# Three-pass expert products in the first layer of a four-layer kernel, with the rounding on VectorE and the rests on GpSimd

## The reference

```python
x = x + _L0_attn_ref(xn, Wqkv, Wproj, bproj, q_scale, k_scale) + _L0_ffn_ref(xn, gate_w, gate_b, expert_w, expert_b)

# in _L0_ffn_ref: combine_w[t, e] is a token's weight for an expert, 0 where it wasn't chosen
expert_out = jnp.einsum('td,edh->teh', x, expert_w) + expert_b[None, :, :]
out = jnp.einsum('te,teh->th', combine_w, expert_out)
```

## Time and profile before

| | before |
|---|---|
| median of 3 runs (lowest to highest) | 1739.81 us (1737.31 to 1744.27) |
| the profiled execution | 1742.57 us |
| its span on the core | 1740.8 us |
| PE busy over the span | 1638.6 us (94%) |
| DVE busy | 1012.4 us (58%) |
| ACT busy | 843.1 us (48%) |
| POOL busy | 396.0 us (23%) |

### The profile page before, as it was taken

One profiled execution on the slowest core, in us unless ns is written; L12 is line 12 of the kernel. 1 busy time (PEld: TensorE's weight loads), 2 busy tenths in 40 slices (PEclk: granted clock), 3 DMA queues, 4 the chain that ended last, 5 costly groups with the idle time before them and its releaser, 6 DMA issues. The chain is left out here.

```text
span 1740.8 us, 22780 instructions
## 1 busy us (share of the span) xinstructions
PE 1638.6 (94%) x8686; PEld 986.4 (57%) x8686; DVE 1012.4 (58%) x1655; ACT 843.1 (48%) x1058; POOL 396.0 (23%) x313
## 2 busy tenths in 40 slices
PE   7799999999889999999999999999999997989887
PEld 4232223223545657877878787877878673434433
DVE  4655555553665454465555555555554547898996
ACT  5667777776434443333434333334434343544543
POOL 1000000000553223030211203030111202755553
PEclk8799999999889999999999999999999998999998
DMA  2322222222107620000000000000000001000000
GB/s 81 52 49 49 50 49 50 50 50 82 47 4 184 154 53 1 2 1 2 1 2 1 1 1 1 2 1 1 1 1 1 1 1 44 1 12 7 6 13 13
DMA packets 20698, 48.78 MB, mean 28 GB/s; under 512 B 1200, under 2 KB 2096, under 8 KB 19824
## 3 DMA queue, kind: packets, MB, share of 16 engines
q1 hardware_dynamic: 20592, 47.34, 11.5%
HBM read 44.84 MB, written 2.36 MB: 27 GB/s over the span
## 5 line engine op out<-in xcount | busy, mean ns | idle before, releaser
L537 ACT ACTIVATE probs<-ps 128x1024 f32<-128x1024 f32 x256 | 245.9, 1024 | 88.1 <-PE ps L793 85.1
L2002 PEld LDWEIGHTS ps_o<-v,probs 128*128 128x128 f32 x2048 | 236.3, 192 | 32.7 <-issue 32.7
L2002 PE MATMUL ps_o<-v,probs 128*128 128x129 f32 x2048 | 246.3, 277 | 1.7 <-ACT probs L1682 1.3
L1682 ACT ACTIVATE probs<-ps_ring 128x1024 f32<-128x1024 f32 x128 | 126.2, 1024 | 197.1 <-PE ps_ring L1983 196.8
L807 PE MATMUL ps<-probs,v 128*32 128x512 f32 x1024 | 136.9, 608 | 0.9 <-DVE o_sb L614 0.9
L1675 ACT ACTIVATE xn<-ps_ring,pack 128x512 f32<-128x512 f32 x64 | 40.6, 685 | 156.6 <-PE ps_ring L1519 156.6
L2195 POOL TENSOR_TENSOR rs<-r,state 128x512 f32<-128x512 f32 x64 | 86.8, 1358 | 92.0 <-DVE state L2363 90.7
L1785 DVE RECIPROCAL rden<-ps_o 128x2 f32<-128x2 f32 x128 | 21.4, 167 | 143.8 <-PE ps_o L2002 143.8
L1772 DVE TENSOR_REDUCE negmax<-ps_ring 128x2 f32<-128x1024 f32 x80 | 94.9, 1219 | 15.2 <-PE ps_ring L1950 15.2
L793 PEld LDWEIGHTS ps<-q_stack,k_stack 32*128 32x128 f32 x512 | 31.5, 185 | 123.5 <-issue 96.2
L2363 DVE TENSOR_TENSOR_SCAN state<-decay,state,kv 128x511 f32<-128x511 f32 x64 | 96.8, 1513 | 6.9 <-issue 1.6
(11 more groups left out here) (423 smaller groups left out, 3436.1 us busy)
## 6 DMA issues: line engine op xcount, KB each, us to landing
cwb<-combine_by_expert SPq DMA_DIRECT2D x8, 2048.0 KB
score<-score_by_expert SPq DMA_DIRECT2D x15, 1024.0 KB, 7.8
pack<-pack_dram SPq DMA_DIRECT2D x1, 3840.0 KB, 15.2
x<-x_in SPq DMA_DIRECT2D x2, 1024.0 KB, 6.0
out<-x SPq DMA_DIRECT2D x8, 256.0 KB, 2.0
pack<-pack_dram SPq DMA_DIRECT2D x1, 1543.0 KB, 6.5
pack<-pack_dram SPq DMA_DIRECT2D x1, 1140.0 KB, 9.3
pack<-pack_dram SPq DMA_DIRECT2D x1, 1088.0 KB, 5.1
```

What stands on the lines that cost most here:

```text
L537: nc.scalar.activation(probs[n % 3][:, 2 * half:2 * half + 2, :], ps, ACT.Exp, scale=float(HD0) ** -0.5).then_inc(read, 1)
L1682: nc.scalar.activation(probs[:, n % 2, m, :, :], ps, ACT.Exp).then_inc(read, 1)
L2002: last = nc.tensor.matmul(ps_o[:, i, k * (D + 1):(k + 1) * (D + 1)], probs[:, (b * PAIRS + p) % 2, m, j, queries], v[:, m, h, :], start=(m ...
```

## The change

From batch 1 on:

- The eight expert products of a batch become three float32r passes each (`split_products`). They stand in twos, in the steps 9, 11, 13 and 15, where there was one in each of the steps 8 to 15.
- The expert weights are split once: ACT copies them rounded (`expert_high`, 128x1024), POOL subtracts (`expert_low`).
- The weighed tokens are split for each product: DVE multiplies and rounds (`xe_high`), in its old places; POOL multiplies again unrounded (into `xe[:, 0]`) and subtracts the rounded part (`xe_low`). Both have four buffers, where `xe` had three.
- The output projection of the batch before moves from step 6 to step 7, ahead of the mean squares.
- The bias product counts in `xe_used` like the others; the load of the next routing weights waits for that count alone.

In batch 0 the products stay as they were.

```diff
@@ sync
                 if b:
-                    sp.wait_ge(xe_ready, b * E0_TRUE)
-                    sp.wait_ge(biased, b)
+                    sp.wait_ge(xe_used, b * (E0_TRUE + 1))
@@ gpsimd
-            for b in range(B):
+
+            def square_qk(b):
                 was_read(pool, ("qk", b))
                 nc.gpsimd.tensor_tensor(sq[:, :, :], qk[:, :, :], qk[:, :, :], ALU.mult).then_inc(squared, 1)
+
+            def rest_of_weighed(b, e):
+                n = b * E0_TRUE + e
+                if e == 0:
+                    pool.wait_ge(cw_loaded, b * 32 + 32)
+                nc.gpsimd.tensor_tensor(xe[:, 0, :], xn[:, at(b)], cwb[:, e, :], ALU.mult)
+                pool.drain()
+                pool.wait_ge(xe_high_ready, n - E0_TRUE + 1)
+                pool.wait_ge(xe_used, used(n - 4))
+                nc.gpsimd.tensor_tensor(single(xe_low[:, n % 4, :]), xe[:, 0, :], xe_high[:, n % 4, :], ALU.subtract).then_inc(xe_ready, 1)
+                pool.drain()
+
+            square_qk(0)
+            pool.wait_ge(exp_out, 1)
+            nc.gpsimd.tensor_tensor(single(expert_low[:, :]), w["expert0"], expert_high[:, :], ALU.subtract).then_inc(padded, 1)
+            for b in range(B):
+                if b + 1 < B:
+                    square_qk(b + 1)
+                for e in range(E0_TRUE if b else 0):
+                    rest_of_weighed(b, e)
@@ scalar
             first_rms(0)
             first_rms(1)
+            nc.scalar.activation(single(expert_high[:, :]), w["expert0"], ACT.Copy).then_inc(exp_out, 1)
             act.wait_ge(exp_in, 1)
@@ vector, weigh
-                if n >= 3:
-                    dve.wait_ge(xe_used, n - 2)
-                nc.vector.tensor_tensor(xe[:, n % 3, :], xn[:, at(b)], cwb[:, e, :], ALU.mult).then_inc(xe_ready, 1)
+                if b == 0:
+                    if n >= 3:
+                        dve.wait_ge(xe_used, used(n - 3))
+                    nc.vector.tensor_tensor(xe[:, n % 3, :], xn[:, at(b)], cwb[:, e, :], ALU.mult).then_inc(xe_ready, 1)
+                else:
+                    dve.wait_ge(xe_used, used(n - 4))
+                    nc.vector.tensor_tensor(single(xe_high[:, n % 4, :]), xn[:, at(b)], cwb[:, e, :], ALU.mult).then_inc(xe_high_ready, 1)
@@ vector, route_probs
-                dve.wait_ge(exp_out, 1)
+                dve.wait_ge(exp_out, 2)
@@ tensor, expert
                 pe.wait_ge(xe_ready, n + 1)
-                nc.tensor.matmul(ps_y[:, :], w["expert0"][:, e * P:(e + 1) * P], xe[:, n % 3, :],
-                                 start=(e == 0), stop=False).then_inc(xe_used, 1)
+                cols = slice(e * P, (e + 1) * P)
+                if b == 0:
+                    nc.tensor.matmul(ps_y[:, :], w["expert0"][:, cols], xe[:, n % 3, :], start=(e == 0), stop=False).then_inc(xe_used, 1)
+                    return
+                if n == E0_TRUE:
+                    pe.wait_ge(padded, 5)
+                split_products(nc, ps_y[:, :], (expert_high[:, cols], expert_low[:, cols]), (xe_high[:, n % 4, :], xe_low[:, n % 4, :]),
+                               start=(e == 0), stop=False).then_inc(xe_used, 1)
@@ tensor, the order
-                    if b and s == 6:
+                    if b and s == 7:
                         output(b - 1)
...
                     if b:
-                        if s >= 8:
+                        if s >= 9 and s % 2 == 1:
+                            expert(b, s - 9)
                             expert(b, s - 8)
```

More of the change, by code:

```diff
@@ L419, in layer0_mix @@
         cwT = sb("cwT", [E0_TRUE, T])
-        xe = sb("xe", [P, 3, T])
+        xe, xe_high, xe_low = sb("xe", [P, 3, T]), sb("xe_high", [P, 4, T]), sb("xe_low", [P, 4, T])
+        expert_high, expert_low = (sb(f"expert0_{part}", [P, E0_TRUE * P]) for part in ("high", "low"))
         lg, rank = sh["logits0"], sb("rank0", [P, NT, E0])
@@ L438, in layer0_mix @@
         o_copied, on_ready = sem("o_copied"), sem("on_ready")
-        xe_ready, xe_used = sem("xe_ready"), sem("xe_used")
+        xe_high_ready, xe_ready, xe_used = sem("xe_high_ready"), sem("xe_ready"), sem("xe_used")
         y_done, x_added = sem("y_done"), sem("x_added")
-        cw_loaded, biased = sem("cw_loaded"), sem("biased")
+        cw_loaded = sem("cw_loaded")
         logits_done, exp_in, exp_out, combined, turned, cw_ready, cw_stored = (
@@ L447, in layer0_mix, with used @@
         block = ctx.enter_context(nc.Block())
+        def used(n):
+            return n // E0_TRUE * (E0_TRUE + 1) + n % E0_TRUE + 1
         def bank1(n):
@@ L825, in expert @@
                 pe.wait_ge(xe_ready, n + 1)
-                nc.tensor.matmul(ps_y[:, :], w["expert0"][:, e * P:(e + 1) * P], xe[:, n % 3, :],
-                                 start=(e == 0), stop=False).then_inc(xe_used, 1)
+                cols = slice(e * P, (e + 1) * P)
[6 more added lines that the diff above has]
+                               start=(e == 0), stop=False).then_inc(xe_used, 1)
             def expert_bias(b):
                 pe.wait_ge(cw_loaded, b * 32 + 32)
-                nc.tensor.matmul(ps_y[:, :], w["expert0_b"][0:E0_TRUE, :], cwT[:, :], start=False, stop=False).then_inc(biased, 1)
+                nc.tensor.matmul(ps_y[:, :], w["expert0_b"][0:E0_TRUE, :], cwT[:, :], start=False, stop=False).then_inc(xe_used, 1)
             def output(b):
```

## The result

The changed kernel takes 1786.38 us in the median of four executions (1764.71 to 1796.86), the kernel before 1741.51 beside it: 1.022 times the time before, interval 1.018 to 1.026 (the ratio leaves out the execution of 1796.86, which stands over 1.5% above the fastest). The forecast was 1760 with a range of 1746 to 1772; the sign was right, the size was not. The profiled execution took 1785.23 us with a span of 1783.4 and a mean granted clock of TensorE of 0.949 (before: 0.966). The execution of 1764.71 us had 0.963, and that is a first hint: the executions differ by how much of the time TensorE ran at its lower clock.

A forecast was written before the change was run, and what follows sets the result against it. PE sets the pace only by a little, with ACT full in steps 8 to 12. Six batches at +2.6 us, +3.0 for the last and +1.7 at the start gave 20.3 us, median 1760, range 1746 to 1772.

The forecast's parts named there:

- part 5: End of the batch: DVE and POOL take turns on SBUF tiles, bringing the batch to +2.6 us.
- the sum: Whole kernel: 6 x 2.6 + 3.0 + 1.7 = 20.3 us slower, median 1760 us.
- Part 1: Expert products, batches 1 to 7: three passes save 17.6 us of PE's work, counting only where PE ends last.
- Part 2: Output projection moved from step 6 to 7: ACT's work up to step 12 comes 0.54 us late.
- Part 3: Experts in twos, steps 8 to 13: ACT sets this stretch, PE's saving is gone, +0.17 us a batch so far.
- Part 4: Steps 14 and 15: POOL's chain to expert 7 makes them 8.5 us where they took 7.53, +1.0 a batch.
- The value 0 for the divide chain: POOL's multiplication for expert 0 beside DVE's divide chain: 0 taken, from a range of 0 to 1.13 us a batch.
- the rival of the divide chain: POOL's multiplication for expert 0 also holds up DVE's divide chain: +1.13 x 7 = 8 us, time 1768; chance 0.14.
- Part 6: Once only: start of attention +1.7 us behind POOL's rest of the weights, last batch paced by POOL +3.0 us.
- Nothing collides: POOL and DVE run side by side in the batches: 8.4 us slower, time 1748; chance 0.13.
- It cancels: Collisions are met by gaps and a faster last batch offsets the batch ends: about 1740; chance 0.06.
- PE's work is what counts: ACT's stretch caught up and POOL's rests in time: 17.6 us come off, time 1722; chance 0.05.

The follow-up runs named there:

- experiment 7: Changed kernel's order with fp32 products of unrounded weighed tokens, no rests and no POOL work in the steps: 1755.46 us, 1.0094 of the kernel before.
- experiment 2: Changed kernel without POOL's rests, the second pass multiplying a tile of zeros: 1744.85 us, 1.0023 of the kernel before.
- 6: Changed kernel with POOL fills in place of its products, plus zero-weight passes on PE ahead of experts 5 and 7: 1763.28 us, 1.0126 of the kernel before.
- 1: Changed kernel plus nine zero-weight PE passes a batch, ahead of experts 5 and 7, where PE waits: 1772.76 us, 1.0178 of the kernel before.
- experiment 8: Changed kernel without POOL's rests, with the output projection back in step 6: 1741.86 us, 1.0025 of the kernel before.
- experiment 12: Kernel before, with only mean squares moved to step 5 and ACT's root steps after steps 5 to 8: 1751.76 us, 1.0075 of the kernel before.
- experiment 5: Changed kernel with both POOL instructions per product replaced by fills of about the same length that read nothing: 1771.52 us, 1.0201 of the kernel before.
- experiment 4: Changed kernel with POOL's rest of the expert weights moved from the start to the begin of batch 1: 1777.88 us, 1.0206 of the kernel before.
- experiment 3: Changed kernel with DVE weighing experts 6 and 7 ahead of the copy of the attention sum: 1764.92 us, 1.012 of the kernel before.
- experiment 9: Changed kernel with one three-pass product in each of steps 8 to 15 and the projection in step 6: 1766.27 us, 1.0181 of the kernel before.

## Why the prediction was wrong in size

For batches 1 to 6, in sums over the six, the steps from one kernel to the next read as a ladder:

| | six batches, us | step |
|---|---|---|
| before | 269.1 | |
| twos and the projection in step 7, fp32 (7) | 276.3 | +7.2 |
| three passes without rests (2) | 271.3 | -5.0 |
| rests without collisions but the cast's (6 less its added passes, by its shortest batch: 6 x 46.3) | 277.8 | +6.5 |
| collisions of DVE and POOL (1, by its shortest batch: 6 x 47.92) | 287.5 | +9.7 |
| the clock (the changed kernel) | 303.9 | +16.4 |

The last step holds all that is left, 0.9 us of another cause among it (part 5); so the clock's share is 14 to 15.5 us.

**The step that failed** is the sum itself: it left the granted clock out. The last part of the prediction named a fall of it in the new wait as something that "would add to it and isn't in the sum", with no price, no chance and no rival of its own. It turned out the largest term: 14 to 15.5 us in batches 1 to 6, and 10.5 - 4.0 = 6.5 or less in batch 7. Without it, the terms measured are 2.5 at the start, 18.4 in the six batches (287.5 - 269.1) and about 4.0 in the last (47.7 - 42.3 - 1.4), 24.9 together against the 20.3 of the sum. On the time before, that is about 1766, and the execution of 1764.71 us at a clock of 0.963 stands there (no trace of it is kept). The rows for a price were at hand in the trace of the kernel before, in batch 0. Two windows, steps 11 to 13 of batch 0 and batches 1 to 7, and PE in time in steps 11 and 12 of batch 0:

```profile
81.00:91.30 10.30, 8.11 (x24) 2.20 (x28) 5.23 (x7) 5.95 (x7) 0.00 (x0) 0.50 0.43 68
102.40:413.70 311.30, 301.38 (x1816) 90.61 (x1812) 158.47 (x188) 238.97 (x248) 11.36 (x6) 1.00 0.27 48
```

```profile
79.44 0.50 PE L793 MATMUL ps<-q_stack,k_stack 32*128 32x512 f32 x2 [1.17 <-ACT probs L537]
...
82.45 0.79 PE L793 MATMUL ps<-q_stack,k_stack 32*128 32x512 f32 x2 [0.91 <-ACT probs L537]
83.17 1.94 PE L807 MATMUL ps<-probs,v 128*32 128x512 f32 x8
```

In batches 1 to 7 the granted clock was 1.00 throughout, also beside two waits of 1.05 and 0.97 us in batch 7, so nothing pointed to a fall there. In batch 0, though, PE waited 1.08, 1.17 and 0.91 us in steps 10 to 12, and the clock fell from 81.0 to 91.3 us: the same value products took 1.94 in place of 1.07. Waits of the size that the sum put into steps 13 to 15 stood beside the lower clock in that trace.

**Part 1** was right that PE's saving counts only where PE ends last, and experiment 7 gives the share: 0.83 of about 2.5 us a batch, and some 1.3 of it in batch 7.

**Part 2** had 0.54 for the moved projection; experiment 8 has 0.44.

**Part 3** was right on ACT's stretch: steps 8 to 12 keep their 3.05 us a step, and what is moved out of them turns up elsewhere (experiment 12). It had step 14 0.17 late. Taken with part 5's 0.3 for expert 5, steps 6 to 13 should have been some 0.5 us longer than before; in batch 4 of the changed kernel they are 1.5 us longer (23.1 in place of 21.6), since PE waits 0.90 us for the rest of expert 5. That is the mis-sized part of the batch's term.

**Part 4**, the chain copy, weigh, rest, product, rest, holds link by link: 8.7 us without collisions where 8.5 was worked out.

**Part 5** holds in kind. The scaling takes 6.3 us in place of 3.5 (ended 230.9 in the working, 7.0 us after its start), weighing 925 in place of 683 ns, POOL's subtraction 1524 ns in the mean. Steps 14 and 15 with collisions were to take 9.6 us and took 9.09; so part 3's miss of 1.0 and this of -0.5 leave the batch at 47.92 in place of 47.45. In the working the first scaling waited for POOL too; it didn't, which is the difference between 7.0 and 6.3.

The value 0 for the divide chain rested on the reciprocals, and these are not hit (1748 ns in the mean, 1749 without POOL's work; in batch 4 a whole multiplication of POOL's, 1.28 us, ran within one of 1.75). By the rule of the Trainium skill ("SBUF — State Buffer", section "Who interferes with whom") that was to be so. The same section says that a VectorE instruction with two SBUF inputs contends with a GpSimd instruction that reads SBUF and not with one that only writes it, while one in a two-port mode, which a cast can enter, contends with GpSimd; experiment 5 agrees on both (750 and 1178 ns beside fills, 749 and 694 without POOL). What the prediction overlooked is the division's product, which has two SBUF inputs. Its mean of 502 in place of 425 ns hides one instruction that met POOL's multiplication for expert 0, in batch 5:

```profile
320.27 1.28 POOL L504 TENSOR_TENSOR xe<-xn,cwb 128x512 f32<-128x512 f32 x1 [3.04 <-DMA cwT<-combine_by_expert]
320.48 1.35 DVE L665 TENSOR_TENSOR on<-nd,rden 128x256 f32<-128x256 f32 x1
```

It took 1.35 us, and step 6 took 3.00 in place of 2.07; in batch 7 such a product took 1.56, and PE's wait for the copy behind it was 2.88 in place of experiment 2's 1.75. So the rival of the divide chain came true in two batches of seven, through the product and not the reciprocal, for about 1 us each.

**Part 6**: the start was 1.7 and is 2.0 on DVE's subtraction (2.68 - 0.69), 2.9 at the first exponential; experiment 4 takes it away. In the profiled execution DVE's scaling ahead of it was already late by 0.57 us, which isn't explained here. The last batch was 3.0, with a bound of +4, and comes to about 4.0: besides the eight rests, the projection, moved out of step 6, no longer covers the wait for the copy there (steps 6 and 7 of batch 7 take 3.65 + 2.49 us in experiment 2, 4.01 + 1.43 before).

**The rivals.** "Nothing collides" is refuted by the scaling's rows. "The divide chain is hit as well" holds for two batches of seven (part 5). "It cancels" is refuted by the time. "PE's work is what counts" is refuted further than it was put: even with rests ready at once (experiment 2) the time is 1.0023 of before, not 1722. It decided on the last rest; experiment 7 shows that the reordering takes 7.2 us before the passes give 5.0.

What stays open: why one batch's end with a wait of 1.24 us keeps its clock (batch 4) and another's with the same wait doesn't (batch 6). Experiments 1 and 6 show that filled waits keep it up. Length alone doesn't decide: in experiment 3 waits of up to 0.92, 1.23 and 0.52 us in steps 13 to 15 stand beside the full clock in all six batches, and in experiment 9 waits of up to 0.99 and 2.24 us in five of six.

## What to carry to other kernels

An edit that takes work from PE and gives PE a wait in its place has a second price, the clock: where the trace has a stretch at the lower clock anywhere, put a price and a chance on a fall in the new wait. Here the length of the wait alone didn't tell whether it came. Before costing a saving on one engine, ask which engine sets that stretch; here even free operands would have gained nothing. And move a helper's work ahead in the order only with an eye on the banks and the instructions it then stands in front of.

## What the runs showed of the hardware

- The clock fell to its lower level at the ends of batches in which PE waited 0.84 to 1.24 us for the last rest (0.84 with the fills, 1.24 in the changed kernel), and rose again within the next batch's first steps: eight value records took 1.76 to 1.94 us in place of 1.06. Nine passes of zero weights a batch kept it at 1.00 in batches 2 to 6 and saved more than they cost (13.6 us in all). Waits as long or longer stood beside the full clock too (1.23 us in experiment 3, 2.24 in experiment 9).
- A fill on POOL, which reads nothing, still holds up DVE's cast (694 to 1178 ns) and not the scaling with two tiles in SBUF (749 and 750 ns).
- DVE and POOL take turns when both have instructions queued that read two tiles in SBUF: in the mean a scaling of 749 ns takes 1340, DVE's subtraction of 1224 takes 2140, and POOL's subtraction, 1.27 to 1.30 us undisturbed, takes 1524 ns.
